# A block of global attention ahead of a six-layer local-attention stack: scores in three rounded passes, two modulation products in other PSUM banks, and fewer loads awaited at the start

## What is computed

```python
mod = (_silu(L0_c) @ L0_wmod).reshape(L0_c.shape[0], 6, 1, -1)
sa, ca, ga, sb, cb, gb = (mod[:, 0], ..., mod[:, 5])
h = _layernorm(x, axis=-1) * (1 + ca) + sa
q = jnp.einsum('bsd,df->bsf', h, Wq) + bq
k = jnp.einsum('bsd,df->bsf', h, Wk) + bk
v = jnp.einsum('bsd,df->bsf', h, Wv) + bv
attn = jax.nn.softmax(jnp.einsum('bqf,bkf->bqk', q, k) * inv_sqrt_d, axis=-1)
x = x + ga * jnp.einsum('bqk,bkf->bqf', attn, v)
h = _layernorm(x, axis=-1) * (1 + cb) + sb
x = x + gb * _L0_ffn_ref(h, ...)
```

## Time and profile before

| | us |
|---|---|
| median of 3 runs | 3269.31 |
| lowest, highest | 3269.1, 3272.2 |
| the profiled execution | 3271.82 |
| its span, first to last instruction | 3270.0 |

### The profile page before, as it was taken

One profiled execution on the slowest core, in us unless ns is written; L12 is line 12 of the kernel. 1 busy time (PEld: TensorE's weight loads), 2 busy tenths in 40 slices (PEclk: granted clock), 3 DMA queues, 4 the chain that ended last, 5 costly groups with the idle time before them and its releaser, 6 DMA issues. The chain is left out here.

```text
span 3270.0 us, 149708 instructions
## 1 busy us (share of the span) xinstructions
PE 3202.3 (98%) x62645; PEld 2538.3 (78%) x62645; DVE 2647.7 (81%) x6351; ACT 2431.3 (74%) x5028; POOL 2213.2 (68%) x1332
## 2 busy tenths in 40 slices
PE   7889999999999999999999999999999999999997
PEld 5668877877887887787787788778788778778875
DVE  5658888878888887888888888888888888888884
ACT  3347777777777777777777778778777777777774
POOL 5448767766776776676776677677677667767762
PEclk9989999999999999999999999999999999999999
DMA  4431111221211131111122111122111122112111
GB/s 160 161 128 51 45 43 43 55 88 48 56 46 42 47 98 48 53 45 43 46 87 63 48 50 46 38 82 71 49 44 48 43 62 87 53 45 53 50 45 37
DMA packets 110574, 200.00 MB, mean 61 GB/s; under 512 B 19280, under 2 KB 40784, under 8 KB 109136
## 3 DMA queue, kind: packets, MB, share of 16 engines
q1 hardware_dynamic: 107168, 185.17, 19.6%
q10 hardware_dynamic: 2736, 5.25, 0.5%
HBM read 41.45 MB, written 23.07 MB: 20 GB/s over the span
## 5 line engine op out<-in xcount | busy, mean ns | idle before, releaser
L438 POOL TENSOR_TENSOR qks<-work 128x1024 f32<-128x1024 f32 x384 | 909.9, 2370 | 134.9 <-issue 125.5
L446 POOL TENSOR_TENSOR qkr<-qks,rnorm 128x1024 f32<-128x1024 f32 x384 | 731.5, 1905 | 310.4 <-issue 223.0
L789 PE MATMUL psum<-wparts,xhi 128*128 128x512 f32 x2304 | 821.8, 438 | 11.9 <-POOL xlo L423 7.0
L573 ACT ACTIVATE sq<-psum 128x512 f32<-128x512 f32 x768 | 459.9, 599 | 301.4 <-PE psum L789 280.4
L454 POOL TENSOR_TENSOR probn<-prob,psumr 128x512 f32<-128x512 f32 x384 | 401.5, 1046 | 370.7 <-DVE psumr L1170 370.5
L1119 DVE TENSOR_REDUCE ssq<-sq 128x8 f32<-128x512 f32 x768 | 519.9, 677 | 4.3 <-ACT sq L573 4.2
L1146 DVE TENSOR_TENSOR work<-psum,rot 128x512 f32<-128x512 f32 x768 | 509.1, 663 | 1.8 <-POOL qks L438 1.8
L814 PEld LDWEIGHTS psum<-kT,qTs 64*32 64x32 f32 x24576 | 360.5, 107 | 145.2 <-issue 129.8
L789 PEld LDWEIGHTS psum<-wparts,xhi 128*128 128x128 f32 x2304 | 384.7, 191 | 101.2 <-issue 50.2
L789 PE MATMUL psum<-wparts,xlo 128*128 128x512 f32 x1152 | 459.7, 399 | 0.0
L1164 DVE TENSOR_REDUCE psumr<-prob 128x8 f32<-128x512 f32 x384 | 261.7, 682 | 243.4 <-ACT prob L625 240.8
(11 more groups left out here) (132 smaller groups left out, 5536.7 us busy)
## 6 DMA issues: line engine op xcount, KB each, us to landing
vsh<-vtok SPq DMA_DIRECT2D x384, 192.0 KB, 2.4
vsh<-vtok SPq DMA_DIRECT2D x384, 64.0 KB, 2.4
wsplit<-wstage SPq DMA_DIRECT2D x15, 1024.0 KB, 6.4
wparts<-wsplit SPq DMA_DIRECT2D x30, 512.0 KB, 3.9
xsh<-xs_in SPq DMA_DIRECT2D x192, 64.0 KB, 2.4
ff_x<-x_mid SPq DMA_DIRECT2D x96, 128.0 KB, 2.4
wraw<-Wqkv_dram SPq DMA_DIRECT2D x18, 512.0 KB, 4.3
rsplit<-rstage SPq DMA_DIRECT2D x5, 1024.0 KB, 3.8
```

The lines of the kernel that those rows point to most:

```text
L438: pool.tensor_tensor(qks[:, :, :], rcos, rsin, ALU.add).then_inc(s["add_ready"], 1)
L446: pool.tensor_tensor(qkr[:, n % 2, :, :], qks[:, :, :], rnorm[:, :].unsqueeze(2).to_broadcast([P, 2 * OCT, DH]), ALU.mult).then_inc(s["qkr ...
L573: act.activation(sq[:, w * OCT:(w + 1) * OCT, :], bank[w].rearrange("p (h n) -> p h n", n=DH), ACT.Square).then_inc(s[("sqq_ready", "sqk_r ...
L789: mm = pe.matmul(out, xparts[xp][:, ti, :], wparts[:, SECTION_AT[w, oc], wp_, :], start=(k == 0), stop=(k == 2))
```

## The change

It does these things:

- q and k of the global stage are kept as two float32r parts each. ACT writes the high part (gq_hi, gk_hi), and a new DVE function projected_low writes the low part from the same PSUM bank, the bias and the high part: four instructions of 128x512 per batch. Scores are three products per half (high by high, high by low, low by high), six per query tile. The parts lie where qT, kgT and hT lay (in x_mid), and hT moves to gel.
- The modulation products go to banks 6 and 7, and PE's wait for mod_ready 2 moves from before the first norm_turn to before project_values of batch 0.
- small_in counts only the condition and the modulation weights. The other three loads count on a new semaphore wa_in, awaited before the first projection. SP issues batches 1 to 3 of x, and all behind them, only once small_in has both.

```diff
+        with ExitStack() as early_qk:
+            qk_parts = [[early_qk.enter_context(nc.sbuf_tensor(f"{name}{half}", [P, S], F32R)) for half in ("_hi", "_lo")]
+                        for name in ("gq", "gk")]
...
-        hT, qT, kgT = (x_mid[:, i * INNER:(i + 1) * INNER] for i in range(3))
+        hT = gel_flat[:, 0:S]
...
             for b in range(B):
+                if b == 1:
+                    sp.wait_ge(s["small_in"], 16 * 2)
                 sp.dma_start(xtok[:, b * TPB:(b + 1) * TPB, :],
...
-            act.dma_start(wa[:, :, :], w_attn).then_inc(s["small_in"], 16)
+            act.dma_start(wa[:, :, :], w_attn).then_inc(s["wa_in"], 16)
...
-            act.wait_ge(s["small_in"], 16 * 5)
+            act.wait_ge(s["small_in"], 16 * 2)
...
             def projected(b, n):
-                dst = (qT, kgT)[n // 2]
                 act.wait_ge(s["gq_ready"], b * 4 + n + 1)
-                act.activation(dst[:, n % 2 * 512:n % 2 * 512 + 512], bank[2 + n], ACT.Identity,
-                               bias=bqk_col[:, n // 2:n // 2 + 1]).then_inc(s["gqk_ready"], 1)
+                act.activation(qk_parts[n // 2][0][:, n % 2 * 512:n % 2 * 512 + 512], bank[2 + n], ACT.Identity,
+                               bias=bqk_col[:, n // 2:n // 2 + 1]).then_inc(s["gqh_ready"], 1)
...
             pe.wait_ge(s["id_ready"], 1)
-            pe.wait_ge(s["mod_ready"], 2)
...
             def project_values(b):
+                if b == 0:
+                    pe.wait_ge(s["mod_ready"], 2)
...
                 for half in range(2):
-                    mm = pe.matmul(bank[i % 2 * 2 + half], qT[:, i * P:(i + 1) * P], kgT[:, half * 512:half * 512 + 512],
-                                   start=True, stop=True)
+                    for k, (xp, wp_) in enumerate(PARTS):
+                        mm = pe.matmul(bank[i % 2 * 2 + half], qk_parts[0][xp][:, i * P:(i + 1) * P],
+                                       qk_parts[1][wp_][:, half * 512:half * 512 + 512], start=(k == 0), stop=(k == 2))
...
+            def projected_low(b):
+                for n in range(4):
+                    hi, lo = (t[:, n % 2 * 512:n % 2 * 512 + 512] for t in qk_parts[n // 2])
+                    dve.wait_ge(s["gqh_ready"], b * 4 + n + 1)
+                    dve.scalar_tensor_tensor(out=lo, in0=bank[2 + n], scalar=bqk_col[:, n // 2:n // 2 + 1], in1=hi.bitcast(F32),
+                                             op0=ALU.add, op1=ALU.subtract).then_inc(s["gqk_ready"], 1)
...
+            projected_low(0)
             values_global(0)
...
                 if b + 1 < B:
+                    projected_low(b + 1)
                     values_global(b + 1)
```

More of the change, by code:

```diff
@@ L188, in build @@
         gsum = sb("gsum", [P, 2, 2])
-        names = """xhi_ready projq_ready projk_ready x_first x_in small_in const_in gain_in ones_ready id_zero id_ready mask_ready pad_ready
+        names = """xhi_ready projq_ready projk_ready x_first x_in small_in wa_in const_in gain_in ones_ready id_zero id_ready mask_ready pad_ready
             silu_step silu_ready wide_ready modp_ready mod_ready gap_ready clamp_step
-            gst_step gmv_ready gve_step grstd_ready gxn_ready gtr_ready gh_ready gq_ready gqk_ready gv_ready gvt_step gvs_ready
+            gst_step gmv_ready gve_step grstd_ready gxn_ready gtr_ready gh_ready gq_ready gqh_ready gqk_ready gv_ready gvt_step gvs_ready
             gs_ready gm_step gm_ready ge_ready gt_ready gte_a gte_d go_ready gri_step gx_ready gout_ready
@@ L469, in _ @@
             act.dma_start(wmod_sb[:, :], wmod).then_inc(s["small_in"], 16)
-            act.dma_start(wa[:, :, :], w_attn).then_inc(s["small_in"], 16)
-            act.dma_start(bqk_col[:, :], b_qk).then_inc(s["small_in"], 16)
-            act.dma_start(bv_row[:, :], b_v.to_broadcast([P, D])).then_inc(s["small_in"], 16)
+            act.dma_start(wa[:, :, :], w_attn).then_inc(s["wa_in"], 16)
+            act.dma_start(bqk_col[:, :], b_qk).then_inc(s["wa_in"], 16)
+            act.dma_start(bv_row[:, :], b_v.to_broadcast([P, D])).then_inc(s["wa_in"], 16)
             act.dma_start(rot_raw[:, :, :].rearrange("p t n -> p (t n)"), rot_tab.rearrange("p t k n d -> p (t k n d)")).then_inc(s["gain_in"], 16)
@@ L478, in _ @@
             act.dma_start(b1_col[:, :, :, :], b1_cols).then_inc(s["const_in"], 16)
-            act.wait_ge(s["small_in"], 16 * 5)
+            act.wait_ge(s["small_in"], 16 * 2)
             act.activation(silu_t[:, 0, :], c_col[:, :], ACT.Exp, scale=-1.0).then_inc(s["silu_step"], 1)
             act.wait_ge(s["modp_ready"], 1)
-            act.activation(mod_col[:, :, :], bank[0][:, 0:6 * B].rearrange("p (k b) -> p k b", b=B), ACT.Copy).then_inc(s["modp_ready"], 1)
+            act.activation(mod_col[:, :, :], bank[6][:, 0:6 * B].rearrange("p (k b) -> p k b", b=B), ACT.Copy).then_inc(s["modp_ready"], 1)
             act.wait_ge(s["mod_ready"], 1)
@@ L688, in _ @@
             pe.wait_ge(s["silu_ready"], 1)
-            pe.wait_ge(s["small_in"], 16 * 5)
+            pe.wait_ge(s["small_in"], 16 * 2)
             for k in range(6):
-                mm = pe.matmul(bank[0][:, k * B:(k + 1) * B], wmod_sb[:, k * D:(k + 1) * D], silu_t[:, 2, :], start=True, stop=True)
+                mm = pe.matmul(bank[6][:, k * B:(k + 1) * B], wmod_sb[:, k * D:(k + 1) * D], silu_t[:, 2, :], start=True, stop=True)
             mm.then_inc(s["modp_ready"], 1)
@@ L694, in _ @@
             for b in range(B):
-                mm = pe.matmul(bank[1][:, b * D:(b + 1) * D], silu_wide[:, b, :], wmod_sb[:, 2 * D:3 * D], start=True, stop=True)
+                mm = pe.matmul(bank[7][:, b * D:(b + 1) * D], silu_wide[:, b, :], wmod_sb[:, 2 * D:3 * D], start=True, stop=True)
             mm.then_inc(s["gap_ready"], 1)
             pe.wait_ge(s["id_ready"], 1)
-            pe.wait_ge(s["mod_ready"], 2)
             def norm_turn(b, which, half):
@@ L716, in project_global @@
             def project_global(b, k):
+                if b == 0 and k == 0:
+                    pe.wait_ge(s["wa_in"], 16 * 3)
                 pe.wait_ge(s["gh_ready"], b * 2 + 2)
@@ L1037, in _ @@
             dve.wait_ge(s["gap_ready"], 1)
-            dve.tensor_copy(ga_row[:, :, :].rearrange("p b d -> p (b d)"), bank[1]).then_inc(s["clamp_step"], 1)
+            dve.tensor_copy(ga_row[:, :, :].rearrange("p b d -> p (b d)"), bank[7]).then_inc(s["clamp_step"], 1)
             steps[0] += 1
```

## The result

| | before | after |
|---|---|---|
| median of 17 runs, us | 3270.31 (3267.05 to 3272.98) | 3263.77 (3261.4 to 3267.58) |
| the profiled execution | 3271.82 | 3261.53 |
| its span | 3270.0 | 3259.2 |

The changed kernel takes 0.998 of the time of the kernel before, with a 95% interval of 0.9973 to 0.9988: 6.5 us less. The forecast was 12.0 less, and 3263.77 lies 0.8 above the range. The profile shows 10.8 less span, but its execution is among the fastest of the changed kernel and that of the earlier trace rows is above the median of its own, so the sum of 6.5 has to be found with several profiles. Two executions, one of the kernel before of 9519 us and one of the changed kernel of 4931 us, lie far above all others and are left out of every ratio and mean.

What follows compares the result with a forecast made beforehand. PE was taken to set the beat of global tiles, with load waits bounding the start and POOL gating later normalizations and the local stage. 9.2 (start) + 3.1 (scores) - 0.3 (low parts) = 12.0 us saved: 3257.3, range 3251 to 3263.

Steps and rivals of the forecast that it cites:

- The start, 4.1 + 3.1: Batch 0's start: silu and PE begin 4.1 us sooner; transposition no longer waits for the gate row, 3.1 us more.
- Rival 4: At the start, late condition, weights or held-back loads give the gain back: 3 to 6 us saved, about 3264.5; chance 0.08.
- The clock in the projections, 2.15: Batch 0's eight projection records: higher clock by the second record, five records 0.43 less each, 2.15 us saved.
- rival 1: Projections stay at 1.2 GHz, 2.15 us missing: 9.9 saved, 3259.4; chance 0.17.
- The gain of a tile, 0.28: Global-stage scores: six passes take 1.40 to 1.48 us against 1.72, saving 0.28 per query tile on PE.
- Which tiles reach the end: Global stage: 11 of 32 tiles count, 3.1 us; the other 21 are hidden, worth 5.9 more without covers.
- DVE's two waits: Idle before DVE's normalization at i = 4 grows to about 1.8 us in batch 1 and 6 in batch 2.
- That the passes' gain stays: Global-stage score gain of 3.1 us, less 0.3 for low parts, counted in the sum; tiles 0 and 1 hidden.
- Rival 2: PE's clock falls in batch 1 around the transpositions, about 2.1 us lost: 9.9 saved, 3259.4; chance 0.15.
- PE's wait before the local stage: At the hand-over to the local stage, PE's idle time grows from 4.05 to 5 us or more.
- Rival 3: Global stage: all 32 tiles reach the end, 9.0 instead of 3.1: 17.9 saved, 3251.4; chance 0.05.
- rival 5: Score passes do not overlap their weight loads, 0.59 us each: 23.6 us slower, 3292.9; chance 0.03.

Runs made afterwards that it cites:

- e9: The kernel before with idle products filling PE's pauses in the global stage (12, 4, 4 at the first turns): 3264.12 us, ratio 0.9981.
- e8: The start part alone, float32 scores, PE's pauses filled with idle products, against the kernel before: 3256.49 us, ratio 0.9959.
- e12: The start part alone with float32 scores and PE's pauses filled, taken again beside e13: 3257.68 us, ratio 0.996 to the kernel before.
- e13: The changed kernel with PE's pauses filled, taken again beside e12: 3252.19 us, ratio 0.9946 to the kernel before.
- e14: The start part alone, float32 scores, POOL's pieces dealt 3, 2, 4, 2, 4, 3, filling only ahead of first turns (14, 4, 4): 3248.25 us, ratio 0.9934.
- e15: The changed kernel with POOL's pieces dealt 3, 2, 4, 2, 4, 3 and filling only ahead of first turns (14, 7, 7): 3243.64 us, ratio 0.9921.
- e2: The scores part alone (float32r parts and three passes) on the kernel before, start as before: 3269.79 us, ratio 1.0.
- e5: The changed kernel with idle products filling PE's pauses in the global stage: 3253.87 us, ratio 0.9949 to the kernel before.
- e6: The changed kernel with the filling of e5 and POOL's pieces dealt 3, 2, 4, 2, 4, 3: 3253.65 us, ratio 0.995 to the kernel before.
- e4: The changed kernel with POOL's weight pieces dealt 3, 2, 4, 2, 4, 3, no filling: 3251.35 us, ratio 0.9945 to the kernel before.
- e11: The changed kernel with POOL's pieces dealt 3, 3, 4, 2, 3, 3 and filling only ahead of first turns (14, 7, 7): 3254.17 us, ratio 0.9946.
- b_again: The kernel before once more, unchanged, for a second profile: 3269.79 us, ratio 0.9998.

## Why the prediction was wrong

- **The sign was right, the range was not**: faster, but by 6.5 us and not 12.0. Another 1.0 us of the distance to 3257.3 is the reference: 3269.31 was a median of three runs, 17 gave 3270.31. The top of the range was also rounded down: its own terms (3261.6, 0.4 and half of 3.1) add up to 3263.6, still below the 3263.77 measured.
- **The start, 4.1 + 3.1: right.** PE started at 7.89 (forecast 8.2) and turned at 12.32 (12.8), and PE did not wait for the gate row. Rival 4 did not occur. With the clock held the start is worth 7.1 us (means 3264.3 in e9, 3257.2 in e8 and e12), with it free 6.9.
- **The clock in the projections, 2.15: the first step that failed, as a size.** It was reasoned that work without pauses since 8.2 would bring the higher clock by the second record. Three profiles of 14 show that, among them the one of the result, which alone would have confirmed the step. Eleven show 5.35 to 6.04 for the eight records, 0.6 less than before on average. This is rival 1, which had 0.17. The term was worth about 1 us in the mean of the profiles.
- **The gain of a tile, 0.28: right** (0.27 over the five tiles of batch 0). By the four-to-three count of the Trainium skill ("FP8 and Floating Point Precision", TensorE Precision Notes) it would have been 0.43; this case's rows do not show that.
- **Which tiles reach the end: the number right where the clock is held, the reason only in part.** Counted were 3.1 less 0.3. The profiles e12 and e13 show 3.5, and DVE's two waits grew, in e13 to 1.01 and 5.20 from 0.65 and 3.82 in e12, by 0.4 and 1.4 where 1.1 and 0.9 were forecast. But POOL was named as the cover of most other tiles, worth 5.9 more without it, and with POOL out of the way e14 and e15 show 4.0. That the count came out is in part luck. PE never waited for a low part.
- **That the passes' gain stays: the second and larger step that failed.** The prediction said of tiles 0 and 1 that they are hidden behind the first row maximum, and stopped there. It should have asked what a longer cover does to PE. At the first turn of batch 1 the pause grew from 3.2 to 3.9, and the slow work behind it costs 1.2 us on six passes and 0.9 on the turn. Rival 2 had this mechanism at one place, around the last turn of batch 1, and 0.15. There it occurs in each of the three profiles of the table with the passes and in none without (1.94 instead of 1.06 or 1.07), with PE idle 0.6 to 1.0 and 2.06 where 0.9 and 2.3 were forecast. Together with the first turn of batch 1, and in some executions those of batches 2 and 3, it takes the whole 2.8 us: with the clock free the passes are worth -1.1 (means 3262.4 and 3263.5, uncertainty 1.8; 0.6 of the loss lies around the span, as below), with it held 4.1. The Trainium skill ("TensorE: Matmul & The Clock Gate", HAM oscillation) says that pauses of PE bring the clock down. The runs agree in direction: filled pauses raise the mean granted clock from 0.9909 to 0.9949.
- **Around the span** the changed kernel takes 2.4 us where that before takes 1.8, so about 0.6 us of the gain is lost outside the profile. e2, e5, e6 and e13 show 2.5 to 2.8, e4 2.1; e11 and e15, with passes too, show 1.8. Counted by the spans alone the passes are worth 5.0 with the clock held (means of the ten runs each), of which 0.9 is lost here. The cause stays open.
- **PE's wait before the local stage** did not grow from 4.05 to 5 but fell to 3.26. It had not been only POOL's last piece: the copy of the first tokens was waited for. Before:

```profile
218.41 0.42 ACT L566 ACTIVATE xhi<-xsh 128x256 fp32r<-128x256 f32 x1 [4.09 <-DMA xsh<-xs_in]
218.90 0.72 POOL L423 TENSOR_TENSOR xlo<-xsh,xhi 128x256 fp32r<-128x256 f32 x1 [1.04 <-ACT xhi L566]
```

After, the same rows have no wait of POOL for it:

```profile
207.73 0.42 ACT L570 ACTIVATE xhi<-xsh 128x256 fp32r<-128x256 f32 x1 [3.04 <-DMA xsh<-xs_in]
...
208.47 0.73 POOL L428 TENSOR_TENSOR xlo<-xsh,xhi 128x256 fp32r<-128x256 f32 x1
```

Rival 3, 9.0 for all tiles, is excluded by e14 and e15 (5.1, uncertainty 1.8), rival 5 by the tile's rows (passes 0.23 apart).

## What to carry to other kernels

When work ahead of a wait gets shorter and the wait ends where it did, the engine's pause gets longer, and on PE that can have a price (here 11 to 15 us more at the lower clock): look behind every such pause for records at the lower clock, before and after. If they are there, products that nobody reads, sized to end just before the awaited event, can give back more than the saved instructions (10 us here, against 4 for the passes), but only where the pause is certain. A term that hangs on when the clock rises should be carried with a chance, not as the likeliest sum, and one profile does not settle it; the mean granted clock of every execution, where it is on record, tells more.

## What the runs showed of the hardware that was not expected

- The clock fell behind pauses of 1.92 us (118.94 in the changed kernel), but stayed up behind one of 3.19 (80.73 in b_again: the turn took 1.09 and the four score records behind it 1.88, full speed). In the second profile of the changed kernel it stayed up behind 1.96 at the same place (122.53, the turn took 1.10). The length of the pause alone does not tell, and neither does one profile: in the first profile of before the same pause was followed by the lower clock, but only from the scores on.
- The same program does the projections at full speed in some executions and not in others: 3.67 and 5.43 us for the same eight records of the changed kernel. The granted clock reads 1.00 in both, so near the start of a program it did not tell; the lengths of the records did.
- Filling PE's pauses with idle products made the kernel before 6 us faster (0.9981), and the changed one 10 (3263.5 to 3253.1 in the mean).
- Time outside the span is 1.8 us in all kernels with float32 scores and 0.3 to 1.0 more in most of those with float32r scores.
